# Edge attention of a four-layer graph network: the low halves are made on GpSimd, and the halves' factor moves into VectorE's product with the adjacency

## The chip, the cores and the metric

The kernel runs on one core of one Trainium2 chip. The metric is the device time of one execution in microseconds (us); less is better. A core has five engines that run their own instruction streams and meet through semaphores: TensorE (PE, with its weight loads shown apart as PEld), VectorE (DVE), ScalarE (ACT), GpSimd (POOL), and SyncE (SP), which here issues all the transfers.

## The reference, cut to what matters

Four layers over 2708 nodes of width 512 share one adjacency matrix; each ends in a layer norm of x plus the layer's output. The change touches layer 2 alone:

```python
node_att = softmax(x @ node_w, axis=0)
h = x @ edge_w
e = h @ h.T
e = where(adj > 0, e, -9e15)
edge_att = softmax(e, axis=1)
combined_att = node_att * edge_att
support = x @ weight
output = adj * combined_att @ support + bias
x = layernorm(x + output)
```

## The kernel before, in words

The 2708 nodes are 22 tiles of 128 rows; the last one has 20. Layer 2 first makes h and the support rows (`project`), and then `edge_attention` goes over the tiles. In code a tile is `(m, u)`, with number `t = 2 * m + u`; `u` picks one of two buffers. The 2708 columns of a tile are cut in three chunks, 1024, 1024 and 660 wide (`CHUNKS`, `c` = 0, 1, 2).

Matrix products take float16 operands, so a float32 value is split in two: a high half, the value times a factor rounded to float16, and a low half, the value times the factor less the high half, rounded again. `P_S` = 1024 is the factor for the attention weights. A product takes three matmuls per pair of blocks: high by high, high by low, low by high.

What happens to a tile, engine by engine:

- PE makes the scores of a chunk in a PSUM slot (two slots for three chunks). In band 0 (tiles 0 to 7) all three chunks are products of h; in band 1 (8 to 15) the first chunk, and in band 2 (16 to 21) the first two, are transposes of scores stored earlier, since e is symmetric.
- DVE masks each chunk (`mask`, L1115) by adding a bias row that it made from the adjacency (`prepare`, L1107, into `edge_bias`), keeping the row maximum, and so frees the slot.
- ACT takes the exponential in place in `edge_scores` (`exp`, L1045).
- DVE multiplies the chunk with the adjacency in place (`weigh`, L1129).
- ACT sums the adjacency row for layer 3 (`sum_degree`, L1075, which uses `edge_part_high` as its output), then writes the high half (`high`, L1054).
- DVE writes the low half into `edge_part_low` (`low`, L1149).
- SP transposes both halves chunk by chunk by DMA (`turn`, L923) into `edge_pt_high` and `edge_pt_low`: high 0, low 0, high 1, low 1, high 2, low 2, in its one queue, ahead of the loads for two tiles on.
- PE multiplies them with the support rows (`products`, L1021). They stand in PE's stream behind the scores of the next tile: scores of t + 1, products of t, scores of t + 2, and so on.
- DVE makes the residual (`finish`, L1159) and its statistics (L408, L410); GpSimd makes x plus bias (`prepare`, L962, into `edge_xb`), and the layer norm's end (`norm.finish`, L419 to L431).

The order on each engine is the order of the code; there is no scheduler. DVE's stream for a tile is mask, weigh, low, the next tile's bias, the scale of the softmax, then `finish` of the tile before.

GpSimd has two instructions of another kind at the start of the stage: the maximum (L971) and the sum (L975) over partitions for the softmax of the node scores. The build puts an instruction that changes GpSimd's configuration, MODIFY_POOL_CONFIG, ahead of each, and another ahead of the first ordinary instruction behind each. DVE's `node_attention` (L1174, L1176) waits for the sum, and tile 1's first mask stands behind it.

Of the kernel before, what the change touches and what calls it, by code (L numbers as in the profile page):

```python
# [18 lines left out]
ALU = mybir.AluOpType  # L19
ACT = mybir.ActivationFunctionType  # L20
# [13 lines left out]
CHUNKS = [(c, min(CHUNK, N - c)) for c in range(0, N, CHUNK)]  # L34
NC = len(CHUNKS)
# [8 lines left out]
X_S, W_S, Q_S, V_S, P_S, O_S = 16.0, 256.0, 16.0, 16.0, 1024.0, 16.0  # L44
# [6 lines left out]
def wait_apart(eng, sem, value, met):  # L51


    if not isinstance(value, int):
        value = eng.to_reg(value)
    eng.wait_ge(met, 1)  # L56
    eng.wait_ge(sem, value)  # L57
# [314 lines left out]
def before(m, u):  # L372

    return (m, 0) if u == 1 else (m - 1, 1)


def is_tile(m, u, t):

    return isinstance(m, int) and 2 * m + u == t
# [431 lines left out]
def edge_attention(nc, layer, x_rows, out_rows, scores_rows, adj_rows, adj, ht, sup, z, bias_row, degree, ident):  # L811
# [3 lines left out]
    with ExitStack() as ctx:  # L815
# [3 lines left out]
        sc = s.sb("scores", [P, 2, N])  # L819
        part = [s.sb(f"part_{a}", [P, NP], F16) for a in ("high", "low")]  # L820
# [16 lines left out]
        pad_high, pad_clear = s.sem("pad_high"), s.sem("pad_clear")  # L837
# [5 lines left out]
        weighed = s.sem("weighed")  # L843
# [4 lines left out]
        part_high = s.sem("part_high")  # L848
# [101 lines left out]
        @block.gpsimd  # L950
        def _(pool):
            nc.gpsimd.memset(part[0][:, N:NP], 0.0).then_inc(pad_high, 1)
            pool.wait_ge(pad_high, 1)
            nc.gpsimd.memset(part[1][:, N:NP], 0.0).then_inc(pad_clear, 1)
            norm.exponent(nc, pool)

            def prepare(m, u):
                t = 2 * m + u
                if not (isinstance(m, int) and m == 0):
                    pool.wait_ge(r_ready, t - 1)  # L960
                pool.wait_ge(xres_loaded[u], 16 * m + 16)
                nc.gpsimd.tensor_tensor(out=xb[:, u, :], in0=xres[:, u, :], in1=bias_row[:, :], op=ALU.add) \  # L962
                    .then_inc(xb_ready, 1)

            def both(m, u):
                prepare(m, u)
                norm.finish(nc, pool, *before(*before(m, u)))

            prepare(0, 0)
            pool.wait_ge(z_max_ready, 1)  # L970
            nc.gpsimd.partition_all_reduce(z_all_max[:, :], z_max[:, :], P, bass.bass_isa.ReduceOp.max) \  # L971
                .then_inc(z_all_max_ready, 1)
            prepare(0, 1)
            pool.wait_ge(z_exp_ready, 1)
            nc.gpsimd.partition_all_reduce(z_all_sum[:, :], z_sum[:, :], P, bass.bass_isa.ReduceOp.add) \  # L975
                .then_inc(z_all_sum_ready, 1)
            both(1, 0)
            both(1, 1)
            pairs(pool, 4, T, both)
            norm.finish(nc, pool, T // 2 - 1, 0)  # L980
            norm.finish(nc, pool, T // 2 - 1, 1)
# [54 lines left out]
        @block.scalar  # L1036
        def _(act):
            def exp(m, u):
                t = 2 * m + u
                for c, (lo, width) in enumerate(CHUNKS):  # L1040
                    if c == 0:
                        act.wait_ge(nmax_ready, t + 1)
                        if not (isinstance(m, int) and m == 0):
                            act.wait_ge(ssum_ready, t - 1)
                    nc.scalar.activation(sc[:, u, lo:lo + width], sc[:, u, lo:lo + width], ACT.Exp,  # L1045
                                         bias=nmax[:, :], accum_out=esum[:, u, c:c + 1]).then_inc(exp_done, 1)

            def high(m, u):
                t = 2 * m + u
                for c, (lo, width) in enumerate(CHUNKS):  # L1050
                    act.wait_ge(weighed, NC * t + c + 1)
                    if c == 0:
                        act.wait_ge(degree_ready, t + 1)
                    nc.scalar.activation(part[0][:, lo:lo + width], sc[:, u, lo:lo + width], ACT.Copy, scale=P_S) \  # L1054
                        .then_inc(part_high, 1)

            def copy_raw(m, u, c, band):

                if c > band:
                    t, (lo, width) = 2 * m + u, CHUNKS[c]  # L1060
                    act.wait_ge(slot_free, NC * t + c + 1)
                    if c == band + 1 and not is_tile(m, u, 0):
                        act.wait_ge(raw_stored, 16 * t)
                    nc.scalar.activation(raw[:, lo - CHUNK:lo - CHUNK + width],
                                         slots[:, (NC * u + c) % 2, 0:width], ACT.Copy).then_inc(raw_copied, 1)

            def sum_degree(m, u):

                t = 2 * m + u
                if not (isinstance(m, int) and m == 0):  # L1070
                    act.wait_ge(adj_loaded[u], 16 * m)
                if not is_tile(m, u, 0):
                    for c in range(NC):
                        act.wait_ge(pt_turned[c], 32 * t)
                nc.scalar.activation(part[0][:, 0:N], adj[:, u, :], ACT.Copy, accum_out=degree[:, bass.ds(t, 1)]) \  # L1075
                    .then_inc(degree_ready, 1)

            def first(m, u):
                for c in range(1, NC):
                    copy_raw(m, u, c, 0)  # L1080
                exp(m, u)
                act.wait_ge(z_all_max_ready, 1)
                nc.scalar.mul(z_neg_max[:, :], z_all_max[:, :], -1.0).then_inc(z_neg_max_ready, 1)
                act.wait_ge(z_neg_max_ready, 1)
                nc.scalar.activation(z_exp[:, :], z[:, :], ACT.Exp, bias=z_neg_max[:, :],
                                     accum_out=z_sum[:, :]).then_inc(z_exp_ready, 1)
                sum_degree(m, u)
                high(m, u)

            def both(m, u, band):  # L1090
                copy_raw(m, u, 1, band)
                copy_raw(m, u, 2, band)
                exp(m, u)
                sum_degree(m, u)
                high(m, u)

            tiles(act, first, both, lambda m, u: None)

        @block.vector
        def _(dve):  # L1100
# [9 lines left out]
            def mask(m, u, c):  # L1110
                t, (lo, width) = 2 * m + u, CHUNKS[c]
                if c == 0:
                    dve.wait_ge(bias_ready, t + 1)
                wait_apart(dve, slot_full, NC * t + c + 1, norm.power_ready)
                nc.vector.tensor_tensor_reduce(  # L1115
                    out=sc[:, u, lo:lo + width], in0=slots[:, (NC * u + c) % 2, 0:width],
                    in1=bias[:, lo:lo + width], scale=1.0 / (Q_S * Q_S), scalar=-3.0e38,
                    op0=ALU.add, op1=ALU.max, accum_out=mx[:, c:c + 1]).then_inc(slot_free, 1)
                if c == NC - 1:
                    dve.wait_ge(slot_free, NC * (t + 1))  # L1120
                    if not is_tile(m, u, 0):
                        dve.wait_ge(exp_done, NC * t)
                    nc.vector.tensor_reduce(out=nmax[:, :], in_=mx[:, :], axis=AX.X, op=ALU.max, negate=True) \
                        .then_inc(nmax_ready, 1)

            def weigh(m, u, c):
                t, (lo, width) = 2 * m + u, CHUNKS[c]
                dve.wait_ge(exp_done, NC * t + c + 1)
                nc.vector.tensor_tensor(out=sc[:, u, lo:lo + width], in0=sc[:, u, lo:lo + width],  # L1129
                                        in1=adj[:, u, lo:lo + width], op=ALU.mult).then_inc(weighed, 1)  # L1130

            def scale(m, u):

# [6 lines left out]
                nc.vector.scalar_tensor_tensor(out=rscale[:, u:u + 1], in0=rinv[:, :], scalar=1.0 / (P_S * V_S),  # L1140
                                               in1=natt[:, bass.ds(t, 1)], op0=ALU.mult, op1=ALU.mult) \
                    .then_inc(rscale_ready, 1)

            def low(m, u, c):
                t, (lo, width) = 2 * m + u, CHUNKS[c]
                dve.wait_ge(part_high, NC * t + c + 1)
                if not is_tile(m, u, 0):
                    dve.wait_ge(pt_turned[c], 32 * t)
                nc.vector.scalar_tensor_tensor(  # L1149
                    out=part[1][:, lo:lo + width], in0=sc[:, u, lo:lo + width], scalar=P_S,  # L1150
                    in1=part[0][:, lo:lo + width], op0=ALU.mult, op1=ALU.subtract).then_inc(part_low, 1)

            def finish(m, u):
                t = 2 * m + u
# [9 lines left out]
            def attend(m, u):  # L1164
                for c in range(NC):
                    mask(m, u, c)
                for c in range(NC):
                    weigh(m, u, c)
                for c in range(NC):
                    low(m, u, c)  # L1170

            def node_attention():
                dve.wait_ge(z_all_sum_ready, 1)
# [269 lines left out]
```

## Time and profile before

| what | value |
|---|---|
| median of 3 runs | 2943.82 us (2940.87 to 2946.68) |
| the profiled execution: its own time / its span | 2943.13 us / 2941.3 us |
| PE busy in the span | 2752.5 us (94%) |
| DVE busy | 1862.5 us (63%) |
| ACT busy | 1553.4 us (53%) |
| POOL busy | 392.8 us (13%) |
| edge attention, from 2073 to 2630 us of the span | some 557 us, 22 tiles |

Every time on a row of the trace counts from the start of the span. A busy engine that has idle time elsewhere is no bound for that reason alone: what counts is which engine the others wait for in the stage that is changed.

### The profile page before, as it was taken

Reading aid. Unit: us, or ns where it says so; the run is one execution under the profiler, and the core shown is the slowest. Engines: PE = TensorE matmul, PEld = TensorE weight load, DVE = VectorE, ACT = ScalarE, POOL = GpSimd, SP = SyncE. Lnnn points to the kernel's source line nnn. Section 1 sums busy time; section 2 is a strip of 40 time slices with the busy share of each in tenths; the row PEclk is TensorE's granted clock in tenths of the full one; section 3 lists DMA queues with packets and bytes.
Section 4 is the critical chain, followed back from the end, with each engine's and each line's share of the span. In section 5 each row is a group of like instructions: output and inputs, shape, how many; then the busy total and the mean of one; then the engine's idle time right before and its main releaser. Section 6 shows DMA issues by size and latency. Waiting matters only on the chain. (4 is left out here: it accounts for less than half of the span.)

```text
span 2941.3 us, 64010 instructions
## 1 busy us (share of the span) xinstructions
PE 2752.5 (94%) x23308; PEld 1788.8 (61%) x23308; DVE 1862.5 (63%) x3387; ACT 1553.4 (53%) x2376; POOL 392.8 (13%) x372
## 2 busy tenths in 40 slices
PE   8989999989989998989899799979899999979998
PEld 6667676767767776767676444457444444434443
DVE  4479897988879798988897322245444555633222
ACT  4467786867768687767687222222343334324222
POOL 0001111111111111111111012300111111210222
PEclk9999999999999999999999899989999999989999
DMA  4221111111111111111110345531455667743454
GB/s 157 81 80 39 39 38 39 38 39 51 48 53 39 39 38 39 38 39 39 44 48 5 129 145 203 198 110 46 115 140 148 185 177 190 201 116 113 172 209 145
DMA packets 220379, 280.58 MB, mean 95 GB/s; under 512 B 138721, under 2 KB 157153, under 8 KB 208865
## 3 DMA queue, kind: packets, MB, share of 16 engines
q1 hardware_dynamic: 220128, 277.13, 30.3%
q8 instruction: 171, 2.80, 0.4%
q14 instruction: 80, 0.65, 0.1%
HBM read 195.39 MB, written 38.44 MB: 79 GB/s over the span
## 5 line engine op out<-in xcount | busy, mean ns | idle before, releaser
L760 DVE SCALAR_TENSOR_TENSOR att_pt_low<-att_ps_t,att_pt_high 128x512 f16<-128x512 f32 (+1 forms) x1056 | 633.5, 641 | 102.0 <-ACT att_pt_high L729 85.8
L729 ACT ACTIVATE att_pt_high<-att_ps_t 128x512 f16<-128x512 f32 (+1 forms) x1056 | 538.6, 559 | 288.6 <-PE att_ps_t L661 286.7
L661 PE MATMUL att_ps_t<-all_ident,att_scores 128*128 128x128 f32 (+1 forms) x3872 | 539.5, 280 | 73.8 <-issue 67.5
L767 DVE CUSTOM_DVE_ANT_0 att_scores<-att_slots,att_adj 128x1024 f32<-128x1024 f32 x528 | 574.2, 1088 | 12.0 <-PE att_slots L673 11.5
L735 ACT ACTIVATE att_scores<-att_scores,att_nmax 128x1024 f32<-128x1024 f32 x528 | 553.8, 1049 | 11.0 <-DVE att_nmax L773 11.0
L673 PE MATMUL att_slots<-l_kk,att_q 128*128 128x512 f16 x2112 | 498.4, 359 | 7.0 <-DMA att_q<-att_q_raw 5.6
L661 PEld LDWEIGHTS att_ps_t<-all_ident,att_scores 128*128 128x128 f32 (+1 forms) x3872 | 410.2, 139 | 110.8 <-issue 74.6
L1276 PE MATMUL a_ps<-l_y,a_adj 128*128 128x512 f16 (+1 forms) x1936 | 431.2, 382 | 9.0 <-DVE a_adj L1290 4.7
L643 PE MATMUL att_ps_pv<-l_vv,att_pt_high 128*128 128x129 f16 (+1 forms) x3872 | 433.6, 221 | 0.4 <-DVE att_pt_low L760 0.4
L643 PE MATMUL att_ps_pv<-l_vv,att_pt_low 128*128 128x65 f16 (+1 forms) x3872 | 403.6, 193 | 0.0
L643 PEld LDWEIGHTS att_ps_pv<-l_vv,att_pt_high 128*128 128x128 f16 (+1 forms) x3872 | 351.6, 98 | 63.5 <-issue 2.5
L643 PEld LDWEIGHTS att_ps_pv<-l_vv,att_pt_low 128*128 128x128 f16 (+1 forms) x3872 | 344.9, 98 | 56.9 <-issue 2.5
L1276 PEld LDWEIGHTS a_ps<-l_y,a_adj 128*128 128x128 f16 (+1 forms) x1936 | 182.9, 98 | 257.3 <-issue 42.1
L1021 PE MATMUL edge_ps_o<-l_sup,edge_pt_high 128*128 128x512 f16 x968 | 288.0, 379 | 0.1
L673 PEld LDWEIGHTS att_slots<-l_kk,att_q 128*128 128x128 f16 x2112 | 202.5, 99 | 126.8 <-issue 7.4
L1260 ACT ACTIVATE a_adj<-l_adj 128x2816 f16<-128x2816 f32 x44 | 112.0, 2550 | 298.7 <-DMA l_adj<-in_adj_cols 277.2
L1007 PE MATMUL edge_slots<-l_ht 128*128 128x512 f16 x1104 | 203.4, 345 | 16.6 <-DVE edge_mx L1115 14.9
L1021 PE MATMUL edge_ps_o<-l_sup,edge_pt_low 128*128 128x512 f16 x484 | 183.3, 379 | 0.0
L1007 PEld LDWEIGHTS edge_slots<-l_ht 128*128 (+1 forms) x1104 | 99.3, 98 | 118.9 <-issue 13.8
L607 POOL TENSOR_SCALAR att_adj<-att_adj 128x2708 f32<-128x2708 f32 x22 | 54.1, 2460 | 816.5 <-DVE att_adj L785 816.5
L1021 PEld LDWEIGHTS edge_ps_o<-l_sup,edge_pt_high 128*128 128x128 f16 x968 | 92.0, 98 | 116.2 <-issue 9.3
L1115 DVE CUSTOM_DVE_ANT_0 edge_scores<-edge_slots,edge_bias 128x1024 f32<-128x1024 f32 (+1 forms) x66 | 71.9, 1097 | 132.6 <-PE edge_slots L1007 128.7
(140 smaller groups left out, 2938.9 us busy)
## 6 DMA issues: line engine op xcount, KB each, us to landing
l_adj<-in_adj_cols SPq DMA_DIRECT2D x44, 1408.0 KB, 6.1
att_adj<-in_adj SPq DMA_DIRECT2D x22, 1354.0 KB, 6.0
l_adj_tiles<-in_adj SPq DMA_DIRECT2D x22, 1354.0 KB, 5.9
p_x_in<-x SPq DMA_DIRECT2D x66, 256.0 KB, 2.6
att_q<-att_q_raw SPq DMA_DIRECT2D x88, 128.0 KB, 2.3
a_xres<-x SPq DMA_DIRECT2D x44, 256.0 KB, 2.7
scores_rows<-edge_raw SPq DMA_DIRECT2D x8, 842.0 KB, 3.4
p_x_in<-in_x SPq DMA_DIRECT2D x22, 256.0 KB, 2.6
```

The source lines that it names most:

```text
L643: mm = nc.tensor.matmul(ps_pv[:, cols], pt[a][0:r, g, (k % GB) * P:(k % GB + 1) * P], vv[0:r, k, h, cols], start=k == 0 and a == 0, stop=k ...
L661: mm = nc.tensor.transpose(ps_t[0:r, g % 2, (k % GB) * P:(k % GB + 1) * P], sp_sb[:, h % 2, k * P:k * P + r], ident[:, :])
L673: mm = nc.tensor.matmul(slots[:, slot, z:z + w], q[:, u, h % 2, a, h // 2, :], kk[:, h, lo + z:lo + z + w], start=a == 0, stop=a == 1)
L729: nc.scalar.activation(pt[0][:, g, 0:w], ps_t[:, g % 2, 0:w], ACT.Copy, scale=P_S) \
L735: nc.scalar.activation(sp_sb[:, b, lo:lo + width], sp_sb[:, b, lo:lo + width], ACT.Exp, bias=nmax[:, b:b + 1]).then_inc(exp_done, 1)
L760: nc.vector.scalar_tensor_tensor(out=pt[1][:, g, 0:w], in0=ps_t[:, g % 2, 0:w], scalar=P_S, in1=pt[0][:, g, 0:w], op0=ALU.mult, op1=ALU.su ...
L767: nc.vector.tensor_tensor_reduce(out=sp_sb[:, h % 2, lo:lo + width], in0=slots[:, (NC * h + c) % 2, 0:width], in1=adj[:, u, lo:lo + width] ...
L1007: mm = nc.tensor.matmul(slots[:, slot, z:z + w], ht[a][:, j, bass.ds(t * P, P)], ht[b][:, j, lo + z:lo + z + w], start=k == 0, stop=k == l ...
L1021: mm = nc.tensor.matmul(ps_o[:, u, :], pt[a][0:r, k, :], sup[b][0:r, k, :], start=k == 0 and a + b == 0, stop=k == T - 1 and a == 1)
L1115: nc.vector.tensor_tensor_reduce(out=sc[:, u, lo:lo + width], in0=slots[:, (NC * u + c) % 2, 0:width], in1=bias[:, lo:lo + width], scale=1 ...
L1260: nc.scalar.activation(a16[:, u, :, :], a32[:, u, :, :], ACT.Copy).then_inc(narrowed, 1)
L1276: mm = nc.tensor.matmul(ps[:, u, :], a16[0:r, u, k, :], y[b][0:r, k, :], start=k == 0 and b == 0, stop=k == T - 1 and b == 1)
```

## The change

DVE's three `low` instructions of a tile are taken out. GpSimd makes the low half instead, as a plain difference of `edge_scores` and `edge_part_high`. For that the factor P_S must be in `edge_scores` already: DVE's product with the adjacency becomes a three-operand instruction (scores times P_S times adjacency), and ACT's high half is a copy without a factor. DVE's first mask of a tile gets a wait for the low halves of the tile two before, whose buffer it overwrites.

```diff
 # GpSimd
+            def low(m, u):
+                t = 2 * m + u
+                for c, (lo, width) in enumerate(CHUNKS):
+                    wait_apart(pool, part_high, NC * t + c + 1, pad_clear)
+                    if not is_tile(m, u, 0):
+                        wait_apart(pool, pt_turned[c], 32 * t, pad_clear)
+                    nc.gpsimd.tensor_tensor(out=part[1][:, lo:lo + width], in0=sc[:, u, lo:lo + width],
+                                            in1=part[0][:, lo:lo + width], op=ALU.subtract).then_inc(part_low, 1)
+
             def both(m, u):
                 prepare(m, u)
                 norm.finish(nc, pool, *before(*before(m, u)))
+                low(m, u)
...
             nc.gpsimd.partition_all_reduce(z_all_sum[:, :], z_sum[:, :], P, bass.bass_isa.ReduceOp.add) \
                 .then_inc(z_all_sum_ready, 1)
+            low(0, 0)
+            low(0, 1)
             both(1, 0)
 # ScalarE, high
-                    nc.scalar.activation(part[0][:, lo:lo + width], sc[:, u, lo:lo + width], ACT.Copy, scale=P_S) \
+                    nc.scalar.activation(part[0][:, lo:lo + width], sc[:, u, lo:lo + width], ACT.Copy) \
 # VectorE, mask
+                    if not (isinstance(m, int) and m == 0):
+                        dve.wait_ge(part_low, NC * (t - 1))
 # VectorE, weigh
-                nc.vector.tensor_tensor(out=sc[:, u, lo:lo + width], in0=sc[:, u, lo:lo + width],
-                                        in1=adj[:, u, lo:lo + width], op=ALU.mult).then_inc(weighed, 1)
+                nc.vector.scalar_tensor_tensor(out=sc[:, u, lo:lo + width], in0=sc[:, u, lo:lo + width], scalar=P_S,
+                                               in1=adj[:, u, lo:lo + width], op0=ALU.mult, op1=ALU.mult) \
+                    .then_inc(weighed, 1)
 # VectorE, low (taken out, with its loop in attend)
-                nc.vector.scalar_tensor_tensor(
-                    out=part[1][:, lo:lo + width], in0=sc[:, u, lo:lo + width], scalar=P_S,
-                    in1=part[0][:, lo:lo + width], op0=ALU.mult, op1=ALU.subtract).then_inc(part_low, 1)
```

GpSimd's stream at the start of the stage before, from the first x plus bias to the third (the plain `ISA` row ahead of another at the same line is the MODIFY_POOL_CONFIG):

```order
L962 TENSOR_TENSOR edge_xb<-edge_xres,all_b_row 128x512
L971 ISA
L971 ISA edge_z_all_max<-edge_z_max 128x1
L962 ISA
L962 TENSOR_TENSOR edge_xb<-edge_xres,all_b_row 128x512
L975 ISA
L975 ISA edge_z_all_sum<-edge_z_sum 128x1
L962 ISA
L962 TENSOR_TENSOR edge_xb<-edge_xres,all_b_row 128x512
```

The same place of the change, where L981 and L985 are the maximum and the sum:

```order
L962 TENSOR_TENSOR edge_xb<-edge_xres,all_b_row 128x512
L985 ISA
L985 ISA edge_z_all_sum<-edge_z_sum 128x1
L971 ISA
L971 TENSOR_TENSOR edge_part_low<-edge_scores,edge_part_high 128x1024 x2
L971 TENSOR_TENSOR edge_part_low<-edge_scores,edge_part_high 128x660
L971 TENSOR_TENSOR edge_part_low<-edge_scores,edge_part_high 128x1024 x2
L971 TENSOR_TENSOR edge_part_low<-edge_scores,edge_part_high 128x660
L962 TENSOR_TENSOR edge_xb<-edge_xres,all_b_row 128x512
```

The low halves of tiles 0 and 1 now stand between the sum's configuration change and the third x plus bias.

DVE's stream from tile 0's product with the adjacency to tile 1's first mask, before:

```order
L1129 TENSOR_TENSOR edge_scores<-edge_scores,l_adj_tiles 128x1024 x2
L1129 TENSOR_TENSOR edge_scores<-edge_scores,l_adj_tiles 128x660
L1149 SCALAR_TENSOR_TENSOR edge_part_low<-edge_scores,edge_part_high 128x1024 x2
L1149 SCALAR_TENSOR_TENSOR edge_part_low<-edge_scores,edge_part_high 128x660
L1107 TENSOR_SCALAR edge_bias<-l_adj_tiles 128x2708
L1174 RECIPROCAL edge_z_rinv<-edge_z_all_sum 128x1
L1176 TENSOR_SCALAR edge_natt<-edge_z_exp,edge_z_rinv 128x22
L1135 TENSOR_REDUCE edge_ssum<-edge_esum 128x1
L1138 RECIPROCAL edge_rinv<-edge_ssum 128x1
L1140 SCALAR_TENSOR_TENSOR edge_rscale<-edge_rinv,edge_natt 128x1
L1115 ISA edge_scores,edge_mx<-edge_slots,edge_bias 128x1024
```

And of the change:

```order
L1143 SCALAR_TENSOR_TENSOR edge_scores<-edge_scores,l_adj_tiles 128x1024 x2
L1143 SCALAR_TENSOR_TENSOR edge_scores<-edge_scores,l_adj_tiles 128x660
L1119 TENSOR_SCALAR edge_bias<-l_adj_tiles 128x2708
L1178 RECIPROCAL edge_z_rinv<-edge_z_all_sum 128x1
L1180 TENSOR_SCALAR edge_natt<-edge_z_exp,edge_z_rinv 128x22
L1150 TENSOR_REDUCE edge_ssum<-edge_esum 128x1
L1153 RECIPROCAL edge_rinv<-edge_ssum 128x1
L1155 SCALAR_TENSOR_TENSOR edge_rscale<-edge_rinv,edge_natt 128x1
L1129 ISA edge_scores,edge_mx<-edge_slots,edge_bias 128x1024
```

The bias row now stands right behind the product with the adjacency; nothing else changed place.

## Rows read from the trace of the kernel before

**Rows 1.** Windows: busy time by engine (count), granted clock, DMA share, GB/s.

```profile
core 0: us, PE busy (x) PEld busy (x) DVE busy (x) ACT busy (x) POOL busy (x), PEclk, DMA share, GB/s
2200.00:2300.00 100.00, 100.00 (x496) 46.31 (x495) 48.68 (x74) 32.37 (x42) 16.42 (x16) 1.00 0.59 162
...
2500.00:2600.00 100.00, 92.61 (x502) 46.90 (x501) 61.89 (x98) 35.82 (x49) 20.52 (x20) 1.00 0.71 183
```

**Rows 2.** Waits in the edge stage: total us, times, longest.

```profile
POOL edge_xb L962 <- DVE edge_residual L1159: 404.5, 20, 23.8
...
DVE edge_residual L1159 <- PE edge_ps_o L1021: 31.8, 22, 12.8
...
PE edge_slots L1007 <- DVE edge_mx L1115: 14.9, 7, 5.8
```

**Rows 3.** Groups by form in the edge stage: busy us, mean ns, idle before.

```profile
L1149 DVE SCALAR_TENSOR_TENSOR edge_part_low<-edge_scores,edge_part_high 128x1024 f16<-128x1024 f32 x44 | 51.9, 1222 | 54.4 <-ACT edge_part_high L1054 54.4
L1129 DVE TENSOR_TENSOR edge_scores<-edge_scores,l_adj_tiles 128x1024 f32<-128x1024 f32 x44 | 51.9, 1222 | 36.2 <-ACT edge_scores L1045 36.2
...
L431 POOL TENSOR_SCALAR edge_x_out<-edge_residual,edge_mv,edge_rstd 128x512 f32<-128x512 f32 x22 | 45.8, 2082 | 4.4 <-POOL edge_rstd L422 4.4
```

**Rows 4.** Timeline of GpSimd at the start of the stage.

```profile
2076.44 1.27 POOL L962 TENSOR_TENSOR edge_xb<-edge_xres,all_b_row 128x512 f32<-128x512 f32 x1 [1.63 <-DMA edge_xres<-x]
2083.28 0.38 POOL L971 PARTITION_ALL_REDUCE edge_z_all_max<-edge_z_max  x1 [5.57 <-issue]
2091.12 2.16 POOL L962 TENSOR_TENSOR edge_xb<-edge_xres,all_b_row 128x512 f32<-128x512 f32 x1 [7.46 <-issue]
2099.31 1.43 POOL L975 PARTITION_ALL_REDUCE edge_z_all_sum<-edge_z_sum  x1 [6.03 <-issue]
2123.30 1.27 POOL L962 TENSOR_TENSOR edge_xb<-edge_xres,all_b_row 128x512 f32<-128x512 f32 x1 [22.56 <-DVE edge_residual L1159]
```

**Rows 5.** Line L962: its configuration changes, ns, first and last start.

```profile
L962 POOLq MODIFY_POOL_CONFIG  x4: 83/83/83, 2083.6 to 2100.7; - x4
```

**Rows 6.** Timeline of DVE, tile 0 to tile 1's first mask.

```profile
2089.79 4.19 DVE L1129 TENSOR_TENSOR edge_scores<-edge_scores,l_adj_tiles 128x1024 f32<-128x1024 f32 x3 [1.72 <-ACT edge_scores L1045]
2095.88 3.12 DVE L1149 SCALAR_TENSOR_TENSOR edge_part_low<-edge_scores,edge_part_high 128x1024 f16<-128x1024 f32 x3 [1.89 <-ACT edge_part_high L1054]
2098.91 1.56 DVE L1107 TENSOR_SCALAR edge_bias<-l_adj_tiles 128x2708 f32<-128x2708 f32 x1
2100.77 0.16 DVE L1174 RECIPROCAL edge_z_rinv<-edge_z_all_sum 128x1 f32<-128x1 f32 x1 [0.30 <-POOL edge_z_all_sum L975]
...
2101.78 1.23 DVE L1115 CUSTOM_DVE_ANT_0 edge_scores<-edge_slots,edge_bias 128x1024 f32<-128x1024 f32 x1
```

**Rows 7.** Groups by form on DVE, 2088 to 2096 us: the third product.

```profile
L1129 DVE TENSOR_TENSOR edge_scores<-edge_scores,l_adj_tiles 128x660 f32<-128x660 f32 x1 | 1.9, 1916 | 0.0
```

**Rows 8.** The same group, 2110 to 2116 us (tile 1).

```profile
L1129 DVE TENSOR_TENSOR edge_scores<-edge_scores,l_adj_tiles 128x660 f32<-128x660 f32 x1 | 0.8, 840 | 0.0
```

**Rows 9.** Timeline of PE, end of tile 1's scores and tile 0's products.

```profile
2094.70 2.54 PE L1007 MATMUL edge_slots<-l_ht 128*128 128x512 f16 x11
2103.07 5.00 PE L1007 MATMUL edge_slots<-l_ht 128*128 128x512 f16 x24 [5.83 <-DVE edge_mx L1115]
2107.91 0.59 PE L1021 MATMUL edge_ps_o<-l_sup,edge_pt_high 128*128 128x512 f16 x2
...
2122.35 13.89 PE L1007 MATMUL edge_slots<-l_ht 128*128 128x512 f16 x72
```

**Rows 10.** Windows of PE there: busy, granted clock, DMA share, GB/s.

```profile
2103.10:2105.00 1.90, 1.90 (x7) 0.50 0.86 164
2105.00:2108.10 3.10, 3.10 (x19) 0.82 0.92 314
2108.10:2112.00 3.90, 3.90 (x19) 1.00 0.80 326
```

**Rows 11.** Issues of transfers, 2097.3 to 2097.6 us: low 0 of tile 0, us to landing.

```profile
edge_pt_low<-edge_part_low SPq DMA_TRANSPOSE x1, 3.2
```

**Rows 12.** Timeline of band 2: DVE, then SP, then PE.

```profile
2498.07 3.12 DVE L1149 SCALAR_TENSOR_TENSOR edge_part_low<-edge_scores,edge_part_high 128x1024 f16<-128x1024 f32 x3 [2.52 <-ACT edge_part_high L1054]
...
2504.34 0.75 DVE L1159 SCALAR_TENSOR_TENSOR edge_residual<-edge_ps_o,edge_rscale,edge_xb 128x512 f32<-128x512 f32 x1 [1.12 <-PE edge_ps_o L1021]
...
2505.72 1.23 SPq L923 DMA_TRANSPOSE edge_pt_low<-edge_part_low  x1
...
2510.96 0.59 PE L1021 MATMUL edge_ps_o<-l_sup,edge_pt_high 128*128 128x512 f16 x2
```

**Rows 13.** Line L923: us to landing, least, median, most.

```profile
DMA to landing us min/median/max: 2.7/3.2/4.9
```

**Rows 14.** The last tile: DVE's low halves, and PEld's wait.

```profile
2604.17 3.12 DVE L1149 SCALAR_TENSOR_TENSOR edge_part_low<-edge_scores,edge_part_high 128x1024 f16<-128x1024 f32 x3 [2.44 <-ACT edge_part_high L1054]
...
2610.54 0.11 PEld L1021 LDWEIGHTS edge_ps_o<-l_sup,edge_pt_high 128*128 128x128 f16 x2 [0.56 <-DMA edge_pt_low<-edge_part_low]
```

More of the change, by code:

```diff
@@ L1142, in scale @@
                     .then_inc(rscale_ready, 1)
[L1144 to L1148, printed above, removed]
-                nc.vector.scalar_tensor_tensor(
-                    out=part[1][:, lo:lo + width], in0=sc[:, u, lo:lo + width], scalar=P_S,
-                    in1=part[0][:, lo:lo + width], op0=ALU.mult, op1=ALU.subtract).then_inc(part_low, 1)
             def finish(m, u):
@@ L1168, in attend @@
                     weigh(m, u, c)
-                for c in range(NC):
-                    low(m, u, c)
             def node_attention():
```

## The prediction

> **What bounds the kernel now.** I read the windows first, to see which engine is full in the stage that is changed. In band 0 (2200 to 2300 us) PE is busy for all of its 100 us and DVE for 48.68; in band 2 it is 92.61 against 61.89 [rows 1]. So PE bounds the stage, and 3 us of work taken off DVE in each tile buys nothing by itself. The waits say where PE stands: over 22 tiles it waits 14.9 us for DVE's masks, of which 5.8 is one wait, while DVE waits 31.8 us for PE at the residual, in each of the 22 tiles [rows 2]. The one long wait is at the start of the stage, so I went to the timelines of that place, engine by engine [rows 4, 6, 9], and then to a tile of band 2 and the last tile, where the slack is least [rows 12, 14].
>
> **The steady tiles.** DVE loses two instructions of 1222 ns and one of 660 columns per tile, 3.12 us together [rows 3, 12]. Its waits for PE show that this time is free already: in band 2 it has finished its other work and waits 1.12 us for the products before the residual [rows 12]. The statistics and the next mask are queued behind that residual, so they don't move when the low halves go, and neither do the short waits of PE for the mask in band 2. Gain: nothing. The product with the adjacency becomes the kind of instruction that the low half was; at 1024 columns both kinds take 1222 ns [rows 3], so nothing there either, and ACT's copy without a factor is the same instruction.
>
> GpSimd now makes the low half. The trace has no such instruction at this width. The nearest is its two-input sum of 512 columns, 1.27 us [rows 4]; in proportion 1024 columns take 2.54 us, and 2.35 if about 0.2 us of the 1.27 is fixed (a choice: no row parts the two). The upper bound is its slowest row, 2082 ns for 512 columns [rows 3], which makes 4.2 us for 1024 and 11.0 for the tile; the lower one is DVE's 1222 ns. I take 2.35, and about 6.3 for the three chunks.
>
> Is that hidden? In band 2 low 0 would end at 2498.07 + 2.35 = 2500.4, be issued to the transpose at once, and land at 2503.6 with the median of 3.2, at 2505.3 with the worst of 4.9 [rows 12, 13]. PE wants it at 2510.96 [rows 12]: slack 5.6 us or more, and 3.8 even at 4.2 us. The last transposed chunk is held by PE's own use of the buffer, and goes out at 2505.72, behind GpSimd's end at 2504.4. The loads behind it in SP's queue therefore move by little. GpSimd itself has 404.5 us of waiting for the residual [rows 2], against 22 times 6.3 = 139 us of new work; x plus bias starts behind the residual, at about 2505.1, just when low 2 is done. DVE's new wait in the mask is for low halves two tiles back, one whole tile old. So the steady tiles cost nothing, with slack on every path.
>
> **The start of the stage.** Here the new instruction has a predecessor that it did not have. Behind each of the two partition reductions GpSimd's configuration is changed back; the two changes stand at 2083.6 and 2100.7 [rows 5]. After the first one the next ordinary instruction starts at 2091.12, after 7.46 us of idleness for which the profile has no releaser [rows 4]. After the second one the next is needed only at 2123.30, and starts without delay [rows 4], so the cost was hidden. In the change the next one is low 0 of tile 0, which DVE made at 2095.88 [rows 6].
>
> First something comes back. The sum over partitions took 1.43 us where the maximum took 0.38 [rows 4]. It started at 2099.31, while DVE wrote the bias row from 2098.91 to 2100.47, and ended 0.27 us behind that [rows 4, 6]. Such blocking shows elsewhere: the sum of 512 columns that began at 2091.12 took 2.16 us for 1.27, and DVE's third product in that stretch took 1916 ns for 840 [rows 4, 7, 8]. In the change the bias row stands where the low half stood and is over by 2095.6, so I take 0.38 us for the sum: ready at 2099.7 in place of 2100.74. Tile 1's first mask then starts 1.05 us earlier, at 2100.7, and PE's third score chunk at 2102.0 in place of 2103.07 [rows 6, 9]. That chunk takes 5.00 us because the granted clock is 0.50 for its first 3 us, that is 1.2 GHz, after 5.83 us of idleness [rows 9, 10]. Starting sooner it meets more of the slow clock: done at about 2107.5, a gain of 0.4 us.
>
> The Trainium skill (SBUF — State Buffer, "Who interferes with whom") says that a DVE instruction with two SBUF inputs and a GpSimd instruction that reads SBUF exclude each other for a whole instruction, as does a DVE one that uses both ports. By that rule the trace agrees: the lost 0.89 and 1.08 us above.
>
> Then the cost. The configuration changes at 2099.7; plus 7.46 us low 0 starts at 2107.2, ends at 2109.5, is issued at 2109.6 and lands 3.2 us later [rows 11], at 2112.8. PE wants it at 2107.5 and before had it in time, starting its products at 2107.91 [rows 9]. So they start 4.9 us later. The two later chunks land by 2118, before their turn.
>
> The second idle stretch, 5.3 us, is about as long as the one that was followed by the half clock. If it falls again, PE's first 3 us of products count half: 1.5 us [rows 10]. Bounds 0 and 1.8.
>
> The least certain term is the 7.46 us, which has one sample. The changes in the other direction cost 5.57 and 6.03 [rows 4], and 1.2 us of the 7.46 lie beside a DVE product [rows 6]; so 5.6 to 7.5.
>
> The Trainium skill (GPSIMD Engine Reference, "2.1 Instruction dispatch") puts about 6 us on the first call after a freshly loaded kernel. The third x plus bias, which starts 0.1 us behind its releaser, shows here that the time runs from the change and not from the call; with 6 us the delay would be 1.5 us less.
>
> What is queued behind low 0: low 1 and low 2 meet tile 1's products on DVE and exclude them in turn, some 2 to 4 us on DVE; the transposes of tile 0 end 12 us later in SP's queue, and with them the loads of tile 2's adjacency (2116 in place of 2104) and ACT's degree sum of tile 1, which waits for all transposes of tile 0. All of this has until PE has done tile 0's products (14.4 us, 2107.91 to 2122.35) and tile 2's scores (13.89) [rows 9], so it stays hidden. As PE is full from there to band 2, the lost time isn't made up.
>
> **The last tile.** PEld waited 0.56 us there for the transposed low 0 [rows 14]. Low 0 comes 2.35 - 1.22 = 1.1 us later. Its landing varies by more than that, so I take 0.5 us, between 0 and 1.1.
>
> **Sum.** 4.9 + 1.5 + 0.5 = 6.9 us more. On the profiled execution's own time, 2943.13, that is 2950.0; the median of the runs is 0.7 us above this execution, so I leave it at 2950.0. It is 0.23%, hardly more than the 0.2% (5.9 us) that a measurement of this kernel can tell from no change.
>
> **The rivals.**
> 1. The reload is shorter or hidden. With 5.6 us low 0 lands at 2111.0, delay 3.0; without a second fall of the clock the sum is 3 to 4 us: 2946.5. For it: a single sample. If the low half didn't wait for any reload it would be about 2943. Chance 0.2.
> 2. GpSimd's difference is much slower than its sum, since it mixes float32 and float16 and rounds. At 4.2 us for 1024 columns the start costs 1.9 more and the last tile 2: 2953.9. The steady tiles still hold. Chance 0.1.
> 3. The two engines exclude each other in the steady tiles. The low halves run at 2498 to 2504; DVE's products, at 2492 to 2495.6, are over then, and its masks read PSUM and one SBUF operand. It would take a loss on the next mask, which PE waits for in band 2: at 1 us in each of 6 tiles 2956, at 1 us in all 22 tiles some 2970. Against it: no two such instructions meet in the timelines but in tile 0 and 1. Chance 0.08; the rule of the SBUF page quoted above is what stands behind this case.
> 4. Faster: DVE's head start reaches PE. The place is the wait of PE for the mask in band 2. It decides if the mask doesn't stand behind the residual, or if the residual waited for DVE; 14.9 us is all that PE waits for masks [rows 2], so 2934 at best. Against it: the residual waits for PE in every tile. Chance 0.04.
>
> My forecast, exposed reload with the fast difference, has the remaining 0.58; its own range is 2946.5 to 2953.
>
> **Numbers.** Slower by over 0.2% is above 2949.7. My forecast gives that in 0.6 of its cases (0.35), rivals 2 and 3 nearly always (0.18), together 0.53. Faster: 0.04. Within: 0.43. The range, 2944 to 2956, takes in the short reload below and the slow difference above, and leaves out the head start and the exclusion in every tile.
>
> **What would show it.** In the changed trace: GpSimd's first low half starts 7 to 8 us behind the sum over partitions, which takes about 0.4 us; PE has two idle stretches at the start, 4.8 us ahead of tile 1's third chunk and about 5 ahead of tile 0's products, the second put down to the transpose of low 0, with a granted clock of 0.50 behind it; a 1024 difference takes 2.3 to 2.6 us; PE is at 100% from 2200 to 2300. I am wrong if the first low half starts by 2103, if PE shows new waits for transposes or masks in bands 1 and 2, or if the difference takes over 4 us.

## The result, and the profile after

| | before | changed |
|---|---|---|
| median of 20 runs | 2944.56 us (2940.87 to 2948.57) | 2949.91 us (2944.75 to 2956.98) |
| ratio to before, 95% interval | | 1.0021 [1.0014, 1.0028] |
| profiled execution: own time / span | 2943.13 / 2941.3 us | 2951.59 / 2949.8 us |

The change makes the kernel slower by about 5.4 us, 2950.0 having been forecast. Executions of one kernel differ by some us ahead of the edge stage (it starts at 2072.96 us in the profile before and at 2077.38 in the one after, in code that is the same). So from here on times in the stage are counted from its first instruction on GpSimd, the memset of `edge_part_high`, called the start of the stage.

The windows of the changed kernel:

```profile
core 0: us, PE busy (x) PEld busy (x) DVE busy (x) ACT busy (x) POOL busy (x), PEclk, DMA share, GB/s
2200.00:2300.00 100.00, 100.00 (x495) 46.12 (x494) 36.98 (x63) 39.68 (x52) 33.18 (x23) 1.00 0.53 147
...
2500.00:2600.00 100.00, 93.59 (x493) 46.14 (x491) 46.08 (x79) 41.46 (x55) 44.40 (x31) 1.00 0.75 198
```

Beside [rows 1]: DVE has lost 12 to 16 us in 100 and POOL has gained 17 to 24, and PE stands as it did. The waits of the stage:

```profile
DVE edge_residual L1165 <- PE edge_ps_o L1033: 146.6, 22, 13.2
...
PE edge_slots L1019 <- DVE edge_mx L1129: 13.4, 7, 3.6
...
PE edge_ps_o L1033 <- DMA edge_pt_low<-edge_part_low: 4.4, 2, 4.0
```

DVE no longer works 3.12 us per tile at the low halves, nor waits for ACT's high halves ahead of them (54.4 us in all [rows 3]). Most of that time has become waiting for PE at the residual, 146.6 us for 31.8 [rows 2]. PE has a new wait, for the transposed low half, of 4.0 us in one piece. GpSimd at the start of the stage:

```profile
2077.38 0.19 POOL L952 MEMSET edge_part_high<- 128x108 f16 x1 [142.80 <-POOLq L169]
...
2095.26 1.31 POOL L962 TENSOR_TENSOR edge_xb<-edge_xres,all_b_row 128x512 f32<-128x512 f32 x1 [7.65 <-issue]
2102.50 0.40 POOL L985 PARTITION_ALL_REDUCE edge_z_all_sum<-edge_z_sum  x1 [5.93 <-ACT edge_part_high L1066]
2109.87 5.59 POOL L971 TENSOR_TENSOR edge_part_low<-edge_scores,edge_part_high 128x1024 f16<-128x1024 f32 x3 [6.97 <-issue]
```

The last row is tile 0's low half: it starts 6.97 us behind the end of the sum, with no releaser, where the same gap was hidden before [rows 4]. ACT's first high chunk had been ready since about 2100.3. Of PE's timeline there, the two rows with an idle stretch in front of them:

```profile
2105.23 6.12 PE L1019 MATMUL edge_slots<-l_ht 128*128 128x512 f16 x24 [3.57 <-DVE edge_mx L1129]
2115.32 1.04 PE L1033 MATMUL edge_ps_o<-l_sup,edge_pt_high 128*128 128x512 f16 x2 [3.97 <-DMA edge_pt_low<-edge_part_low]
```

And PE's windows behind the second wait (busy, granted clock, DMA share, GB/s):

```profile
2115.30:2120.70 5.40, 5.38 (x13) 0.50 0.92 177
2120.70:2132.40 11.70, 11.70 (x54) 1.00 1.03 271
```

Beside [rows 9, 10]: the wait for the mask is shorter, 3.57 us for 5.83; then comes the new wait, 3.97 us; then 5.4 us at the granted clock of 0.50. PE's products of tile 0 start 37.94 us behind the start of the stage (2115.32 - 2077.38) against 34.95 before (2107.91 - 2072.96): 3.0 us. The first residual stands at 55.17 against 49.49: 5.7 us. From the first residual to the last it takes 503.77 us against 502.65: 1.1 us.

### The profile page after: what moved, and what is told of

It is laid out like the page before. It is cut to its first block and busy times, and to the rows that moved or that the text cites. A ratio compares the mean times of both kernels' runs of the same rounds, so it can differ in the third digit from the quotient of the medians.

```text
span 2949.8 us, 64168 instructions
## 1 busy us (share of the span) xinstructions
PE 2759.8 (94%) x23308; PEld 1792.9 (61%) x23308; DVE 1797.8 (61%) x3321; ACT 1552.5 (53%) x2376; POOL 514.9 (17%) x438
## 5 line engine op out<-in xcount | busy, mean ns | idle before, releaser
L971 POOL TENSOR_TENSOR edge_part_low<-edge_scores,edge_part_high 128x1024 f16<-128x1024 f32 (+1 forms) x66 | 124.6, 1917 | 280.6 <-ACT edge_part_high L1066 273.6
```

What stands on the lines that cost most here:

```text
L971: nc.gpsimd.tensor_tensor(out=part[1][:, lo:lo + width], in0=sc[:, u, lo:lo + width], in1=part[0][:, lo:lo + width], op=ALU.subtract).then ...
```

## The experiments

Three numbers go with each: the first residual from the start of the stage, the time from the first residual to the last, both from the profiled execution, and the ratio to the kernel before, from timed runs of both on the same chip. The first number scatters: in the five profiles in which the order up to the first residual is that of before (before, 1, 3, 6 and 10) it is 48.91 to 50.21. So a difference of about 1.3 us or less in that column shows nothing by itself.

| kernel | first residual | first to last | ratio, 95% interval |
|---|---|---|---|
| before | 49.49 | 502.65 | |
| changed | 55.17 | 503.77 | 1.0021 [1.0014, 1.0028] |
| 1 tile 0 on VectorE | 50.21 | 504.24 | 1.0003 [0.9994, 1.0012] |
| 2 only tile 0 on GpSimd | 54.48 | 504.78 | 1.0031 [1.0018, 1.0043] |
| 3 factor only | 48.91 | 502.65 | 0.9996 [0.9987, 1.0005] |
| 4 reordered | 43.07 | 504.38 | 0.9978 [0.9968, 0.9988] |
| 5 deferral, low on VectorE | 48.47 | 502.60 | 1.0004 [0.9995, 1.0013] |
| 6 each low half twice | 49.31 | 505.01 | 1.0009 [1.0000, 1.0018] |
| 7 bias row ahead | 47.83 | 503.12 | 0.9997 [0.9988, 1.0006] |
| 8 order on VectorE alone | 42.96 | 502.95 | 0.9965 [0.9952, 0.9978] |
| 9 reordered, last tile on VectorE | 43.03 | 502.54 | 0.9968 [0.9955, 0.9980] |
| 10 no added wait | 49.26 | 502.38 | 0.9992 [0.9983, 1.0001] |
| 11 changed, deferral only | 54.74 | 503.96 | 1.0016 [1.0008, 1.0025] |

**1. Is it tile 0?** The changed kernel with tile 0's low half on VectorE:

```diff
-            low(0, 0)
             low(0, 1)
...
+                for c in range(NC):
+                    vector_low(m, u, c)      # in first(): VectorE, tensor_tensor subtract
```

> As the changed kernel, but tile 0's low half is made on VectorE (a plain difference); the other 21 stay on GpSimd. Theory A (the loss is GpSimd's configuration change in front of tile 0's low half): the first residual stands 49.5 us behind the start of the stage, as before, the ratio to the kernel before is 0.9995 to 1.0007 (about +1 us from the last tile). Theory B (every tile costs something on GpSimd): first residual as before too, but the 21 tiles behind it stay 3 us or more longer than before, and the ratio stays at about 1.002.

The ratio is 1.0003, and the first residual is back to 50.2. Twenty-one of 22 low halves are still on GpSimd. Theory A, as the text above calls it, holds; the 1.6 us in the tiles behind (504.24 against 502.65) are looked into in experiments 6, 9 and 10.

**2. The mirror image.** Tile 0 on GpSimd, the other 21 on VectorE.

> The mirror image: only tile 0's low half on GpSimd, the other 21 on VectorE. Theory A: first residual 55 us behind the start of the stage, ratio 1.0015 to 1.0025, nearly the whole loss of the change. Theory B: ratio under 1.0007.

GpSimd's timeline of this kernel:

```profile
2106.96 6.57 POOL L971 TENSOR_TENSOR edge_part_low<-edge_scores,edge_part_high 128x1024 f16<-128x1024 f32 x3 [7.29 <-issue]
```

The gap is there again, 7.29 us, and PE waits 5.2 us for low 0. One low half of 22, on the wrong side of the configuration change, costs what the whole change costs: 1.0031 lies above the 1.0015 to 1.0025 expected, but its interval [1.0018, 1.0043], from six runs, overlaps the change's. The first residual is 54.48, for 55 expected. The 504.78 behind it holds a stretch at the half clock at 2536 us that no other profile here has; no cause for it was found.

**3. The factor alone.**

```diff
-                nc.vector.tensor_tensor(out=sc, in0=sc, in1=adj, op=ALU.mult)
+                nc.vector.scalar_tensor_tensor(out=sc, in0=sc, scalar=P_S, in1=adj, op0=ALU.mult, op1=ALU.mult)
-                nc.scalar.activation(part[0], sc, ACT.Copy, scale=P_S)
+                nc.scalar.activation(part[0], sc, ACT.Copy)
-                nc.vector.scalar_tensor_tensor(out=part[1], in0=sc, scalar=P_S, in1=part[0], ...)
+                nc.vector.tensor_tensor(out=part[1], in0=sc, in1=part[0], op=ALU.subtract)
```

> Only the factor is moved: VectorE's product with the adjacency carries P_S, ScalarE copies without it, and VectorE itself makes the low half as a plain difference. Both theories: 1222 ns for the product and for the difference at 1024 columns, ratio within 0.0007 of 1. If the change of instruction kind costs anything, its mean would be longer than 1222 ns.

Of DVE's groups by form in this kernel, the product:

```profile
L1129 DVE SCALAR_TENSOR_TENSOR edge_scores<-edge_scores,l_adj_tiles 128x1024 f32<-128x1024 f32 x44 | 53.0, 1246 | 36.2 <-ACT edge_scores L1045 36.2
```

The plain difference takes 1221 ns. The product's mean is 1246 and not 1222, which was not expected; the excess over 44 instructions is 1.1 us, and tile 0's three products alone took 4.20 us for 3.12, as before in another of the three [rows 6, 7]. So it is that one collision with x plus bias, not the kind of instruction. The stage is as long as before.

**4. Both waits taken away.** On GpSimd tile 0's low half goes ahead of the sum; on VectorE the node factor and tile 0's scale go behind tile 1's product:

```diff
             prepare(0, 1)
+            low(0, 0)
             pool.wait_ge(z_exp_ready, 1)
...
-            low(0, 0)
             low(0, 1)
...
+                if is_tile(m, u, 1):
+                    node_attention()
+                    scale(0, 0)
                 scale(m, u)
```

> The changed kernel with two things reordered: GpSimd makes tile 0's low half ahead of the sum over partitions, and VectorE takes the node scores' factor and tile 0's scale behind tile 1's product instead of ahead of tile 1's masks. Theory A: PE's wait for tile 1's first mask (3.6 us in the change, 5.8 before) and its wait for tile 0's low half (4.0 us) both go, and with them the stretch at the half clock; first residual 41 to 44 us behind the start of the stage against 49.5 before and 55.2 in the change; ratio to the kernel before 0.9970 to 0.9985. Theory B: the ratio stays above 1.

```profile
2067.99 27.60 PE L1019 MATMUL edge_slots<-l_ht 128*128 128x512 f16 x144 [1.68 <-PEq L169]
2096.46 0.60 PE L1033 MATMUL edge_ps_o<-l_sup,edge_pt_high 128*128 128x512 f16 x2 [0.87 <-DMA edge_pt_low<-edge_part_low]
```

PE's timeline runs through the scores of tiles 0 and 1 without a stop, 144 matmuls in 27.60 us, and waits 0.87 us for low 0. The first residual is at 43.07, 12.1 us ahead of the change, and the granted clock is 1.00 from 2067.9 to 2112. Ratio 0.9978. Two things were moved at once here; experiment 11 takes them apart.

**5. The deferral without GpSimd.**

> The kernel before (low halves on VectorE), with only the deferral of the node scores' factor and tile 0's scale behind tile 1's product. Tile 1's first mask then waits for nothing but VectorE's own stream (low half, bias row), which ends at about 2100.5 on the clock of before: 1.3 us gained on PE's wait of 5.8 us, ratio 0.9990 to 1.0000. If it gains as much as the reordered GpSimd version, the freed VectorE has no part in that gain; if it gains clearly less, the difference is what moving tile 0's low half off VectorE is worth once the configuration change is out of its way.

PE's wait for tile 1's mask is 4.6 us, as expected, and the first residual is at 48.47, less than half a us below the five of the order of before. A gain isn't shown: the ratio, 1.0004 [0.9995, 1.0013], is above the 0.9990 to 1.0000 expected, and can't be told from 1. The low half and the bias row still stand ahead of the mask.

**7. The bias row ahead of the low half**, on VectorE, in the kernel before.

> The kernel before with one thing moved: VectorE writes tile 1's bias row ahead of tile 0's low half, not behind it. If the sum over partitions was held up by the bias row (1.43 us before, 0.40 in the change), it takes about 0.4 us here and tile 1's first mask starts 1 us earlier. If it was the low half that slowed GpSimd, or if the length of the sum belongs to it, it stays at 1.4 us. Ratio within 0.0007 of 1.

GpSimd's timeline of this kernel:

```profile
2100.88 0.53 POOL L975 PARTITION_ALL_REDUCE edge_z_all_sum<-edge_z_sum  x1 [5.82 <-issue]
```

The sum takes 0.53 us, so the 1.43 us of [rows 4] don't belong to it. But the low half isn't without effect on it either: alone the sum takes 0.40, and here it started inside the low half's second chunk. Experiments 3 and 5 leave the bias row where it was, and their sums, which start 25.1 us behind the start of the stage where that of before starts at 26.35, end ahead of the bias row, after 0.41 and 0.47 us. So the 1.43 us is what one execution had: there the sum came late enough to start inside the bias row. PE's wait for the mask is 4.0 us here, against 5.44 in experiments 1, 3, 6 and 10.

**8. All of the gain on VectorE.** The kernel before, no low half on GpSimd. Tile 0 goes product, bias row, tile 1's first mask, low half; the deferral as in 4.

```diff
                 for c in range(NC):
                     weigh(m, u, c)
+                if is_tile(m, u, 0):
+                    prepare(*after(m, u))
+                    mask(0, 1, 0)
                 for c in range(NC):
                     low(m, u, c)
```

> The kernel before, GpSimd without any low half; on VectorE the bias row and tile 1's first mask stand ahead of tile 0's low half, and the node scores' factor is deferred as in the fourth experiment. If the gain of the reordered version (0.9978) is all a matter of PE's wait at tile 1's first mask, this one has it too: no wait of PE for that mask, about 1 us for tile 0's low 0, first residual 42.5 to 43.5 us behind the start of the stage, ratio 0.9970 to 0.9985. If the low halves on GpSimd are part of the gain, it stays above 0.999.

0.9965 [0.9952, 0.9978], a little below the 0.9970 to 0.9985 expected, and the first residual at 42.96: the same as with GpSimd's help. The freed VectorE has no part in the gain. The profiled stage is 6.2 us shorter than before (49.49 + 502.65 against 42.96 + 502.95); the medians of that chip, 2934.56 and 2946.33, lie further apart. In the profiles of experiments 4, 8 and 9 the stage also starts earlier, at 2068.0 to 2069.0 us, than in the ten others (2071.3 to 2077.8), though the code ahead of it is the same. Whether that is chance, and what makes up the rest, wasn't found.

**6. Is there slack in the steady tiles?** Experiment 1, with each low half on GpSimd written twice.

> Tile 0 on VectorE as in the first experiment, and each of the other low halves is written twice on GpSimd, one after the other with a wait between (11.5 us of low-half work per tile in place of 5.8). The output is the same. Theory A (the steady tiles have slack of 5 us and more for low 0): the first residual as before; low 0 of each tile 2.2 us later; the tiles between the first and the last residual lengthen by under 2 us, ratio to the kernel before 1.000 to 1.001. Theory B: GpSimd's work per tile is already exposed, so doubling it adds some us more in band 2; ratio above 1.002.

GpSimd's groups by form, tiles 2 to 21, the first and the second writing:

```profile
L972 POOL TENSOR_TENSOR edge_part_low<-edge_scores,edge_part_high 128x1024 f16<-128x1024 f32 x40 | 86.3, 2157 | 163.8 <-ACT edge_part_high L1069 163.8
...
L975 POOL TENSOR_TENSOR edge_part_low<-edge_scores,edge_part_high 128x1024 f16<-128x1024 f32 x40 | 85.1, 2128 | 5.7
```

Nearly 6 us more work per tile lengthen the tiles by 0.8 us in all (505.01 against 504.24 in experiment 1), and that is the last tile, where PE waits 1.74 us for low 0 against 0.97. In the other tiles PE's waits are those of experiment 1 (9.8 us for masks in both, none for transposes).

**10. The wait that was added to the mask.** The residual of the tile two before already stands ahead of that mask on DVE, and it implies that the low half has been made.

```diff
                 if c == 0:
                     dve.wait_ge(bias_ready, t + 1)
-                    if not (isinstance(m, int) and m == 0):
-                        dve.wait_ge(part_low, NC * (t - 1))
```

> The first experiment (tile 0 on VectorE, the rest on GpSimd) without the added wait in the mask. PE's waits for masks behind 2140 us go from 9.8 us back to 9.1; the last tile still waits about 1 us for low 0. If the 9.8 stays, it isn't the added wait. Ratio within 0.001 of 1.

PE's waits behind 2140 us in this kernel:

```profile
PE edge_slots L1018 <- DVE edge_mx L1126: 9.0, 6, 1.7
```

9.0 us against 9.8 with the wait and 9.1 before. So a wait that is always met costs 0.7 to 0.8 us in all: beside experiment 1 it is 0.1 us or less in each of five masks, and 0.42 in that of the last tile (PE waits 1.61 us there with the wait, 1.19 without). In the last tile the time is lost ahead of the statistics' last instruction (L410), which stands before the mask on DVE, 0.47 us for 0.11; why isn't shown. First to last residual: 502.38. The second half of the expectation failed: GpSimd makes the last tile's low half here too, and yet PE doesn't wait for it (PEld 0.42 us).

**9. Reordered, last tile on VectorE, no added wait.**

> The reordered version with the last tile's low half back on VectorE and without the added wait in the mask (the residual in front of the mask implies it). The tiles from the first to the last residual took 504.4 us in the reordered version and 502.65 before; if the difference is the added wait (0.35 us in each mask that PE waits for) and the last low half (0.5 to 1.1 us), they take 502.5 to 503.2 here. Ratio to the kernel before 0.9970 to 0.9982.

502.54 us from first to last, as before, and 0.9968 [0.9955, 0.9980]. It can't be told from experiment 8. Since experiment 10 has 502.38 with the last low half on GpSimd, nothing here shows that its place matters.

**11. The change with the deferral alone.**

> The changed kernel with VectorE's deferral alone; GpSimd's order as in the change, so the configuration change still stands in front of tile 0's low half. If that is what sets the start, PE gets tile 1's first mask without a wait, and then waits for the transposed low 0 the longer: 8 to 9 us in one piece, first residual 51 to 55 us behind the start of the stage, ratio 1.0005 to 1.0020. If the two waits of PE were one cause, both shrink and the ratio falls below 0.999.

```profile
2111.91 1.04 PE L1033 MATMUL edge_ps_o<-l_sup,edge_pt_high 128*128 128x512 f16 x2 [10.57 <-DMA edge_pt_low<-edge_part_low]
```

PE's two waits have become one of 10.57 us, more than the 8 to 9 expected, and it ends 38.2 us behind the start of the stage (2111.91 - 2073.70), as in the change (37.9). As long as the configuration change stands in front of low 0, nothing that VectorE does earlier reaches PE. Experiment 4 is this kernel with one line moved, tile 0's low half ahead of the sum: that alone takes the first residual from 54.74 to 43.07 and the ratio from 1.0016 to 0.9978.

## Why the prediction was right, point by point

**The steady tiles cost nothing, gain nothing.** Right but for the mask's new wait, below. PE is at 100% from 2200 to 2300, and doubling GpSimd's work adds nothing there. The freed 3.12 us per tile went into the wait for the residual.

**The reload in front of tile 0's low half.** Right as a mechanism, shown from three sides: experiment 1 takes tile 0's low half away from it and the loss goes; experiment 2 leaves only that one on GpSimd and the loss stays; from experiment 11 to 4 it moves to the other side of the sum and more than the loss comes back. Its sizes: gap 6.97 us for 7.46 forecast; the 1024 difference 2.16 us for 2.35; landing 3.2 for 3.2. The sum was ready at 25.5 us from the start of the stage (2102.90) for the 26.7 forecast. Together these bring the landing of low 0 1.9 us earlier than forecast, so that the products started 3.0 us late for 4.9.

**The second fall of the clock.** The term was mis-sized the other way: 5.4 us of work at the half clock is 2.7 us lost, beyond the bound of 1.8. I had counted only 3 us of slow work, as in the stretch of [rows 10]. Even the first stall had more in the change: tile 1's third chunk ran at 0.50 from 2105.2 to 2110.5 and took 6.12 us for 5.00, which cost nothing, as low 0 came later still. The two errors nearly cancel: 3.0 + 2.7 = 5.7 us at the first residual, for 6.4 forecast.

**The sum over partitions.** It took 0.40 us for the 0.38 forecast, but PE's wait for the mask fell to 3.57 us and not to 4.8. What the base had besides the long sum is a late one: GpSimd's x plus bias ended 20.32 us behind the start of the stage in the profile before [rows 4], and at 19.19 in the change and in all eleven experiments. The sum starts 25.1 us behind the start of the stage in the change, for 26.35 before. So this part of the base was one execution's, and the mask came 1.2 us sooner than forecast.

**The mask's new wait.** Costed at nothing because the low halves that it waits for are one tile old. They are; but with the wait in the code PE waits 0.7 us more for masks over the stage (experiment 10). This step was wrong, and small.

**The last tile.** 0.5 us forecast. PEld's wait went from 0.56 to 0.97 us and PE's own is 0.48 in the change, 0.97 in experiment 1. As forecast, but not to be told from scatter: PE waits 0.54 and 0.52 us there in experiments 7 and 8, with the low half on VectorE, and not at all in experiment 10, with it on GpSimd.

**The rivals.** The short reload is out (6.97, 7.29 and 7.14 us in front of low 0 in the change and experiments 2 and 11), as are the slow difference (2158 ns) and a head start of DVE. The bound of 2934 given for that one doesn't follow from the 14.9 us: 2943.1 less 14.9 is 2928.2. The exclusion in steady tiles doesn't happen: from tile 2 on no low chunk of the change takes more than 2.13 us. In tile 1 it does, the three chunks taking 6.94 us together for the 5.59 of tile 0; and in experiment 6, where GpSimd works longer, two chunks of band 2 took 2.93 and 2.40.

The sum was 6.9, the profiled stage moved 6.8, the medians 5.4 (4.1 to 8.2 by the interval). That the forecast time lies 0.1 us from the measured one is luck twice over. The base, 2943.1, lies 1.4 us below the median of 20 runs before, which makes up for a sum 1.5 above the move. And within the sum three terms were off with both signs: the delay 1.9 us too long, the slow clock 1.2 too short, the tiles behind 0.6 too short (1.1 for 0.5, the mask's wait and the last tile).

## What to carry to other kernels

Before an instruction is moved to an idle engine, look at what stands ahead of it there in the stream: an engine that is 13% busy can still have one stretch in which it can't serve, and only the first use meets it. If PE is full, freeing another engine gives nothing; the idle stretches of PE itself, here 5.8 us at the first mask of tile 1, are where time is, and a matter of order alone (experiment 8: 6.2 us of the profiled stage, 0.35% by the timed runs). A base taken from one execution can hold a delay that no other one has, here 1.1 us in front of the sum. When a stall is priced, price the work at the lower clock behind it too, by its own length and not by that of the last stall.

## What the runs showed of the hardware

The gap behind a configuration change of GpSimd differs by direction. Over the 13 profiles it is 5.5 to 6.0 us ahead of a partition reduction, and 6.7 to 7.7 us ahead of the next ordinary instruction where that one stands right behind. It does not start when that instruction is wanted: before, the third x plus bias is wanted 22 us behind the change and starts 0.1 us behind its releaser [rows 4]. Nor is its length fixed. In experiments 4 and 9 the low half of tile 1 was wanted 2.5 and 2.3 us behind the sum, when its high half was ready, and started 9.8 and 9.9 us behind it:

```profile
2112.55 5.61 POOL L971 TENSOR_TENSOR edge_part_low<-edge_scores,edge_part_high 128x1024 f16<-128x1024 f32 x3 [9.78 <-issue]
```

(This row is of experiment 4.) PE didn't wait for it there; what made the gap longer isn't known.

A reduction over partitions is held up by VectorE, also by instructions with two SBUF inputs. In six profiles the sum started inside a VectorE instruction: inside the bias row before, inside the second of tile 0's three low chunks in experiments 1, 5, 7, 8 and 10. It took 0.46 to 1.43 us, and each time it ended 0.26 or 0.27 us behind the end of that instruction. In experiment 8:

```profile
2094.15 1.20 POOL L975 PARTITION_ALL_REDUCE edge_z_all_sum<-edge_z_sum  x1 [5.92 <-issue]
```

VectorE's second chunk started at 2093.87 and took 1.22 us, so that it ended at 2095.09; the sum ended at 2095.35. With no such instruction beside it a reduction takes 0.38 to 0.40 us.
